# Filling the slot table of a mixture-of-experts kernel: 64 indirect scatters to device memory, or one-hot products summed on TensorE

## What is computed

```python
s_raw_MN = x_MD @ Wg_DN                                   # 8192 tokens x 8 logits
routed = softmax(s_raw_MN[:, :7]);  shared = softmax(s_raw_MN[:, 7:])
_, idx_MK = lax.top_k(routed, 1)                           # one routed expert per token
mask = sum(one_hot(idx_MK, 7), axis=1)
sel = routed * mask;  routed_n = sel / sum(sel, axis=-1)   # its gate
gates = concatenate([routed_n, shared / sum(shared)])
for each expert e:                                         # w1: 256 x 1024, w2: 512 x 256
    a, b = split(x_MD @ w1[e]);  y += gates[:, e] * ((silu(b) * a) @ w2[e])
x = x + gb * y
```

## Time and profile before

| what | value |
|---|---|
| median of three runs | 3036.81 us |
| the profiled execution's own time | 3036.99 us |
| its span in the profile | 3035.2 us |
| busy: PE, DVE, POOL, ACT | 75%, 67%, 65%, 44% of the span |
| last store of `shared_program` issued | 2466.2 us after the start of the span |
| first instruction of DVE in `routing_program` | 2469.96 us |
| first copy of `cur` in `experts_program` | 2579.56 us |

### The profile page before, as it was taken

One profiled execution on the slowest core, in us unless ns is written; L12 is line 12 of the kernel. 1 busy time (PEld: TensorE's weight loads), 2 busy tenths in 40 slices (PEclk: granted clock), 3 DMA queues, 4 the chain that ended last, 5 costly groups with the idle time before them and its releaser, 6 DMA issues. The chain is left out here.

```text
span 3035.2 us, 29143 instructions
## 1 busy us (share of the span) xinstructions
PE 2270.4 (75%) x7448; PEld 1053.1 (35%) x7449; DVE 2030.8 (67%) x2297; ACT 1321.1 (44%) x2151; POOL 1980.8 (65%) x816
## 2 busy tenths in 40 slices
PE   4677687687687786786786785349889940899998
PEld 3223233233232232232232231125555520565664
DVE  3298998998998898988988989924444440122222
ACT  1465565565565665655655655402222210222221
POOL 0189989989889889899898899900000017455553
PEclk7778788787787787787787786669999975999999
DMA  3333433433333434334333333151111100222221
GB/s 109 74 74 75 97 81 73 98 84 73 88 79 81 91 78 90 81 71 101 79 80 91 88 82 85 36 215 63 48 55 62 62 22 2 83 84 86 83 87 51
DMA packets 113435, 238.40 MB, mean 79 GB/s; under 512 B 21516, under 2 KB 75534, under 8 KB 100752
## 3 DMA queue, kind: packets, MB, share of 16 engines
q1 hardware_dynamic: 93328, 189.86, 25.7%
q0 software_dynamic: 14368, 36.00, 4.1%
q10 hardware_dynamic: 5600, 11.01, 1.0%
HBM read 106.10 MB, written 39.20 MB: 48 GB/s over the span
## 5 line engine op out<-in xcount | busy, mean ns | idle before, releaser
L721 POOL TENSOR_TENSOR hs<-hs,c_rep 128x2048 f32<-128x2048 f32 x256 | 1154.6, 4525 | 69.4 <-ACT state L560 69.2
L555 ACT ACTIVATE dA<-d_rep,a 128x512 f32<-128x512 f32 x1024 | 683.6, 686 | 621.8 <-DVE hs L641 618.0
L641 DVE TENSOR_TENSOR_SCAN hs<-dA,state,hs 128x512 f32<-128x512 f32 x768 | 914.6, 1263 | 27.1 <-ACT dA L555 25.9
L714 POOL TENSOR_TENSOR hs<-u_rep,b_rep 128x2048 f32<-128x2048 f32 x96 | 433.6, 4516 | 104.7 <-PE y_ps L437 97.4
L628 DVE TENSOR_TENSOR hs<-u_ps,b_rep 128x2048 f32<-128x2048 f32 x160 | 364.6, 2280 | 135.9 <-PE u_ps L427 135.5
L396 PE MATMUL bank<-xin,w_in 128*128 128x512 f32 x512 | 342.9, 826 | 91.2 <-ACT xpad L491 86.3
L437 PE MATMUL y_ps<-hs,gather 128*32 128x512 f32 x2048 | 275.4, 686 | 142.1 <-POOL hs L721 142.1
L407 PE MATMUL bank<-xdbl,w_dt 65*128 65x512 f32 x256 | 181.5, 847 | 174.9 <-DVE delta L617 117.8
L641 DVE TENSOR_TENSOR_SCAN hs<-dA,hs 128x512 f32<-128x512 f32 x256 | 289.8, 1202 | 12.0 <-ACT dA L555 12.0
L822 POOL TENSOR_TENSOR rstd<-var,mhalf 128x4 f32<-128x4 f32 x16 | 16.1, 1007 | 411.2 <-DVE var L924 411.2
L427 PE MATMUL u_ps<-us,spread 32*128 32x512 f32 x320 | 222.2, 782 | 72.8 <-POOL us L704 62.0
(11 more groups left out here) (169 smaller groups left out, 2646.9 us busy)
## 6 DMA issues: line engine op xcount, KB each, us to landing
d_rep<-delta SPq DMA_DIRECT2D x256, 256.0 KB, 4.3
u_rep<-us SPq DMA_DIRECT2D x384, 64.0 KB, 2.2
b_rep<-bc_rows SPq DMA_DIRECT2D x64, 256.0 KB, 4.4
c_rep<-bc_rows SPq DMA_DIRECT2D x64, 256.0 KB, 7.3
xin<-in_x SPq DMA_DIRECT2D x16, 512.0 KB, 3.8
xres<-in_x SPq DMA_DIRECT2D x16, 512.0 KB, 3.6
x<-xres SPq DMA_DIRECT2D x16, 512.0 KB, 4.4
x_sb<-x SPq DMA_DIRECT2D x16, 512.0 KB, 4.3
```

Of the source, the lines that this page charges most:

```text
L555: nc.scalar.activation(dA[:, u % ABANK, :], d_rep[:, q % 2, j, :], ACT.Exp, scale=t["a"][:, u:u + 1]).then_inc(da_ready, 1)
L641: nc.vector.tensor_tensor_scan(hs[:, s % RING, g, :], dA[:, u % ABANK, :], hs[:, s % RING, g, :], state[:, u:u + 1] if m else 0.0, ALU.mul ...
L714: nc.gpsimd.tensor_tensor(hs[:, s % RING], u_rep[:, i % UBUF, :].unsqueeze(1).to_broadcast([P, NG, T]), b_rep[:, par, :].rearrange("p (g t ...
L721: nc.gpsimd.tensor_tensor(hs[:, s % RING, :, :], hs[:, s % RING, :, :], c_rep[:, par, :].rearrange("p (g t) -> p g t", g=NG), ALU.mult).th ...
```

## The change

Nothing of the list in device memory is left: not its tensor, nor the store of empties (L812), its wait and the two memsets in `shared_program`, nor the 64 scatters and the load in `routing_program`. In their place:

- DVE makes two one-hot tiles of each column of tokens: `at_lane`, 128x128 (row p is 1 at the lane of the slot of token p), and `at_tile`, 128x70 (1 at its slot tile). `sel` holds `at_tile` times the token number plus one, made by DVE, and `at_tile` times the gate, made by ACT (64 activations with the gate as a scale): 128x140 together. This goes in eight groups of `GR` = 8 columns: DVE has three instructions per group, 128x560, 128x1024 and 128x560.
- PE sums `at_lane`, as weights, times `sel` over the 64 columns in one bank of PSUM (`placed`, 128x2x70): lane by slot tile, token number plus one and gate. A group's products begin when both `id_ready` (DVE) and `gate_ready` (ACT) have come to it.
- DVE makes `meta` from `placed`, in five instructions instead of three. An empty slot has 0 there and becomes `EMPTY`.

The chain ahead is written anew with the same results. The first true entry of each token comes from one running sum over 448 elements that is set back to zero at each token (`keep_e`) and one comparison, in place of 13 instructions. `one`, `prefix` and `total` are laid out expert by expert, so that the sums over the columns are one scan of 448 elements (`keep_j` sets it back) instead of seven of 64, and `more` is one instruction instead of seven. `total` is multiplied first and signals alone. `owner` moves behind the eight groups and takes three instructions instead of eight.

```diff
 shared_program
-            sp.wait_ge(empty_set, 2)
-            sp.dma_start(slots_dram.rearrange("(p k) w -> p k w", p=P), empty[:]).then_inc(slots_set, 16)
-            sp.wait_ge(slots_set, 16)
...
-            nc.gpsimd.memset(empty[:, :, 0], EMPTY).then_inc(empty_set, 1)
-            nc.gpsimd.memset(empty[:, :, 1], 0).then_inc(empty_set, 1)
...
 routing_program, gpsimd
             nc.gpsimd.memset(below[:], 1.0).then_inc(tri, 1)
+            nc.gpsimd.memset(keep_e[:], 1.0).then_inc(tri, 1)
+            nc.gpsimd.memset(keep_j[:], 1.0).then_inc(tri, 1)
...
-            pool.wait_ge(slots_ready, 1)
-            pool.wait_ge(consts, 5)
-            for j in range(NTILE):
-                nc.gpsimd.indirect_dma_start(slots_dram, bass.IndirectOffsetOnAxis(slot[:, j:j + 1], 0), info[:, j, :], None).then_inc(scattered, 16)
-        @block.sync
-        def _(sp):
-            sp.wait_ge(scattered, 16 * NTILE)
-            sp.dma_start(slots[:], slots_dram.rearrange("(p k) w -> p k w", p=P)).then_inc(loaded, 16)
-            sp.wait_ge(loaded, 16)
...
 scalar, behind the exponential
+            for g in range(NGRP):
+                act.wait_ge(at_ready, g + 1)
+                for j in range(GR * g, GR * g + GR):
+                    last = nc.scalar.activation(sel[:, j, 1, :], at_tile[:, j, :], ACT.Copy, scale=gate[:, j:j + 1])
+                last.then_inc(gate_ready, 1)
...
 tensor
-            nc.tensor.matmul(flat(prefix), below[:], flat(one), start=True, stop=True)
             nc.tensor.matmul(flat(total), ones[:], flat(one), start=True, stop=True).then_inc(counted, 1)
+            nc.tensor.matmul(flat(prefix), below[:], flat(one), start=True, stop=True).then_inc(counted, 1)
+            for j in range(NTILE):
+                if j % GR == 0:
+                    pe.wait_ge(id_ready, j // GR + 1)
+                    pe.wait_ge(gate_ready, j // GR + 1)
+                last = nc.tensor.matmul(flat(placed), at_lane[:, j, :], sel[:, j].rearrange("p a b -> p (a b)"),
+                                        start=(j == 0), stop=(j == NTILE - 1))
+            last.then_inc(all_placed, 1)
...
 vector
-            link(v.tensor_copy(taken[:], mask[:, :, 0]))
-            link(v.tensor_copy(one[:, :, 0], mask[:, :, 0]))
-            for e in range(1, NR - 1):
-                link(v.tensor_tensor(one[:, :, e], mask[:, :, e], taken[:], ALU.is_gt))
-                link(v.tensor_tensor(taken[:], taken[:], mask[:, :, e], ALU.max))
...
+            dve.wait_ge(consts, 8)
+            link(v.tensor_tensor_scan(flat(cum), flat(keep_e), flat(mask), 0.0, ALU.mult, ALU.add))
+            v.scalar_tensor_tensor(out=one[:].rearrange("p e j -> p j e"), in0=cum[:], scalar=1.0, in1=mask[:],
+                                   op0=ALU.is_equal, op1=ALU.mult).then_inc(onehot, 1)
...
+            link(v.tensor_tensor_scan(flat(incl), flat(keep_j), flat(total), 0.0, ALU.mult, ALU.add))
+            link(v.tensor_tensor(more[:], by_expert(each128), incl[:, :, NTILE - 1:NTILE].to_broadcast([P, NR, NTILE]), ALU.is_lt))
...
+            link(v.tensor_reduce(pos[:], part[:].rearrange("p e j -> p j e"), AX_X, ALU.add))
...
+            for g in range(NGRP):
+                at = slice(GR * g, GR * g + GR)
...
+                v.tensor_tensor(at_tile[:, at], among(kidx, SLOT_TILES), spread(tile, SLOT_TILES), ALU.is_equal).then_inc(at_ready, 1)
+                v.tensor_tensor(at_lane[:, at], among(lanes, P), spread(lane, P), ALU.is_equal)
+                dve.wait_ge(at_ready, g + 1)
+                v.tensor_tensor(sel[:, at, 0, :], at_tile[:, at], spread(id1, SLOT_TILES), ALU.mult).then_inc(id_ready, 1)
...
+            dve.wait_ge(all_placed, 1)
+            link(v.tensor_scalar(empty[:], placed[:, 0, :], 0.5, float(EMPTY), ALU.is_lt, ALU.mult))
+            link(v.scalar_tensor_tensor(out=meta[:, :, 2], in0=placed[:, 0, :], scalar=-1.0, in1=empty[:], op0=ALU.add, op1=ALU.add))
+            link(v.tensor_scalar(meta[:, :, 0], meta[:, :, 2], float(BATCH * SEQ - 1), None, ALU.min))
+            link(v.tensor_copy(meta[:].bitcast(F32)[:, :, 3], placed[:, 1, :]))
```

More of the change, by code:

```diff
@@ L1000, in routing_program @@
[L1000 to L1003 removed]
+        ex, p, mask, cum, work = (sb(n, [P, NTILE, NR]) for n in ("ex", "prob", "mask", "cum", "work"))
@@ new lines, in routing_program @@
+        keep_e, keep_j = sb("keep_e", [P, NTILE, NR]), sb("keep_j", [P, NR, NTILE])
+        nt, tend, base, own, reach = sb("nt", [P, NR]), sb("tend", [P, NR]), sb("base", [P, NR]), sb("own", [P, SLOT_TILES]), sb("reach", [P, SLOT_TILES, NR])
+        at_lane = sb("at_lane", [P, NTILE, P])
+        at_tile, sel = sb("at_tile", [P, NTILE, SLOT_TILES]), sb("sel", [P, NTILE, 2, SLOT_TILES])
+        empty = sb("empty", [P, SLOT_TILES])
+        prefix, total = (ctx.enter_context(nc.psum_tensor(n, [P, NR, NTILE], F32)) for n in ("prefix", "total"))
@@ L1093, in _ @@
             link(v.tensor_scalar(base[:], base[:], float(P), None, ALU.mult))
[L1095 to L1099 removed]
+            link(v.tensor_tensor(part[:], incl[:], total[:], ALU.subtract))
```

88 lines of the change are left out of this document (41 added, 47 removed).

## The result

The changed kernel takes **2970.73 us** (median of four runs, 2970.52 to 2972.13), the kernel before 3036.80 (3034.68 to 3037.05) beside it: ratio 0.9786, interval 0.9775 to 0.9798. That is 66 us less. The forecast was 2969.8. The profiled execution's own time is 2970.52, against a forecast of 2970.0.

A forecast was written before the change was run, and what follows sets the result against it. The serial chain from the shared expert's last stores through list to `cur` bounds it. Parts 1 to 4 save 5.7 us; with the table, `cur` moves 67.0 earlier: 3036.99 to 2970.0, median-adjusted 2969.8; range 2965.5 to 2977.5.

The forecast's parts named there:

- Part 1: Start of the routing block: removing the store of empties gives 0.2 us, at most 0.43; five more POOL constants cost nothing.
- Part 2: One-hot choice on DVE: one scan and one wide instruction, 4.27 to 2.04 us, with 0.28 per 256-byte jump.
- Part 3: Gate: `total` signals alone, so DVE's wait for PE goes; 3.48 becomes 2.40 us, 1.08 less.
- Part 4: Counts, from the scan of `total` to the table: 10.34 becomes 8.12 us, small instructions at 0.265 each.
- Part 5: Table: DVE sets the pace at 2.41 us per group (bound 2.81), ACT 2.05, PE 2.18; before, it took 84.0.
- start at half clock: PE's first table group at half clock takes 3.94 us, later ones 2.18; PE catches up 0.23 per group.
- rival in which the clock stays at half through all products: PE sets the table's pace at 3.94 us per group: 12.3 us more, 2982.1; 9 in 100.
- `meta` to `cur`: From the finished table to the experts' first POOL instruction: 1.62 us, unchanged.
- The experts: Routed experts, from first `cur` to the end: 455.6 us as before; another value would show the forecast wrong.
- term that it left out: PE's clock staying up until the experts' first transpose: taken as nothing, bound 2.0 us less.
- ACT's pace: Rival: ACT sets the table's pace at 3.0 us per group; 4.9 us more, 2974.7; 8 in 100.
- table loads: Slower rival: ACT loads its table ahead of each copy, 1.54 us per copy; 3049 us; 1 in 100.

The follow-up runs named there:

- warm variant: The changed kernel plus nine spare 448-column products on PE ahead of the table, which nobody reads; 2971.13 us, ratio 0.9784.
- spare DMA: The changed kernel plus one unread GpSimd indirect gather of 128 rows in the routing block, issued early (2969.89 us) or, in a second run, late (2966.2 us).
- extra drain: The changed kernel with smaller last groups and one GpSimd drain behind the routed experts' last gather; 2960.65 us, ratio 0.9753.
- small groups, warm: The changed kernel with groups of 8 (six times), 6, 4, 3 and 3 columns, plus nine spare PE products ahead of the table; 2971.51 us.
- table alone: The changed kernel with the old chain (expert by expert, both products ahead of the signal), one-hot table kept; 2974.77 us, ratio 0.9802.

## Why the prediction was right

**What bounds it**: right. The list was all that the experts waited for; every us of the serial stretch came off the whole.

**Part 1**, 0.2: measured 0.25, of which the store alone is 0.16. The five constants more were free: the last began at 2473.06, three us ahead of DVE's scan at 2476.11. Even the margin was larger than thought, since the `affine_select` takes 0.29 now, not 0.71.

**Part 2**, 2.04: measured 2.08. The scan of 448 took 1.09 (1.07 forecast). The open question was whether a *write* with a jump of 256 bytes pays what a read does. It does: 0.92 for `one` (L1078) and 0.93 for its reader, where the unjumped kind takes 0.62 to 0.63. (L1078 is of another kind than the products, SCALAR_TENSOR_TENSOR, but at 128x512 the kernel before has this kind at 680 ns, L617, and the product at 687, L963.) The Trainium skill's rule (SBUF — State Buffer, "Door 1: The DMA port swizzle"), by which every access that crosses to a new line pays, agrees in all three places, L1099's 0.91 among them.

**Part 3**, 2.40: measured 2.46. DVE no longer waits for `total`.

**Part 4**, 8.12: measured 7.76. The mis-sized term are the small instructions: 0.265 each was forecast, while they stand 0.20 to 0.23 apart.

**Part 5.** The group: 2.41 forecast, 2.44 measured (0.65 + 1.14 + 0.65 from start to start, where the records are 0.73, 1.22 and 0.73 long). The choice between 2.41 and 2.81 was made by the pair of the earlier trace rows, and the trace bears it out. The Trainium skill's rule (VectorE: DVE Perf Modes, "The DRAIN you can't avoid") would have had 2.81 by its main sentence, that the next instruction waits until the pipe is empty; the same section adds that one that is not held starts earlier, which the prediction left out. The trace agrees with the addition: unlinked instructions begin some 0.08 us before the one ahead has ended.

ACT: eight copies 2.05 forecast, 2.06 measured, though for another reason than I gave: one copy's record is 339 ns, near the upper price of 0.345, but they start 0.245 apart. The gain of running on, which the prediction named, is there (0.09 per copy), and it cancels what the record is longer than forecast. That the scale is what makes the record longer no run shows, since none has the same copy without it. ACT stays 0.38 under DVE.

PE: 2.18 per group at full clock. A group with a pause ahead of it takes 2.15, but groups that follow each other without a pause start only 1.91 apart (2498.26, 2500.17, 2502.08). The other step that was mis-sized is the **start at half clock**. "I take the first group at half", 4.0 us. The windows (PE, weights, DVE, ACT and POOL busy; granted clock; DMA):

```profile
2491.40:2497.40 6.00, 6.00 (x26) 6.00 (x27) 6.00 (x8) 5.01 (x20) 0.00 (x0) 0.50 0.00 1
2497.50:2508.00 10.50, 10.50 (x88) 10.31 (x86) 10.50 (x15) 8.98 (x37) 0.00 (x0) 1.00 0.00 0
```

The clock stood at 0.50, 1.2 GHz, for 6 us after 9.8 us in which PE had been idle, and then went to 1.00, 2.4 GHz. In the variants it rose 3.6 to 6 us behind the first product, with no cause that the rows tell apart. 26 records went through at half clock instead of 16. So PE was behind by 2.5 us instead of 1.8 (3.94 - 2.18), but caught up 0.53 per group (2.44 - 1.91) instead of 0.23. By the prediction's own price of a group the later rise would have lain on the path; that it did not is luck, two mis-sized terms against each other. The warm variant shows that it cost nothing: same end. Had the table been two groups shorter, 0.3 us would have been on PE's path, by the debt left behind the sixth group. The rival in which the clock stays at half through all products did not come: ahead of the last group and in the warm variant there are pauses of 0.3 us, and the clock stays at 1.00.

The wait of DVE for `placed`, "1 us": 1.19. `owner` was hidden.

**`meta` to `cur`**, "1.62, which stays": this step failed. (1.62 is itself 0.03 short: `meta`'s last row ends at 2577.91, not 2577.94.) It was 0.53, and the missing 1.1 was GpSimd's drain after 64 scatters. The prediction had looked at every instruction that was removed, and not at what the barrier behind it was waiting for.

**The experts**, 455.6: 456.16. The first gather takes 1.23 instead of 1.01 now that no scatter goes ahead of it; before, the first scatter had paid this (1.29 in the earlier trace rows). The spare DMA that took this away brought no fall that could be told from the spread of the stretch over versions with the same code, 455.00 to 456.71. The kept traces show what goes with that spread: PE's granted clock is at 0.50 when the experts start and rises to 1.00 some 13 to 16 us behind `cur`, and over the thirteen traces without the extra drain the stretch grows by 0.50 us for each us that the rise comes later. The ends are 455.0 with the rise 12.9 behind `cur` (small groups, warm) and 456.7 with 16.5 (table alone). Before, it came 14.35 behind `cur`, after, 15.58: 0.6 us by this slope, which is all of the 0.5. So by its own sign, "if the experts' stretch is not 455.6", the prediction was off here by 0.5, by a moment of the clock that no row explains. The term that it left out, a clock that stays up until the first transpose, was nothing, as it took: between 2520 and 2525 the granted clock was 0.50.

So the 0.9 us between forecast and result is partly luck. Chain 0.3 and `meta` to `cur` 1.1 better; table 0.3, experts 0.5 and the store 1.27 worse. These sum to -1.4 + 2.1 = +0.7, and the forecast had rounded `cur` up by 0.1: the 0.5 us by which the profiled time missed, within rounding. The largest two, the drain at 1.1 and the store at 1.27, nearly cancel, and neither was foreseen. Of the rivals, ACT's pace (a group of 3.0) and table loads (none: each copy 0.339) are excluded by the rows above.

## What to carry to other kernels

A long row of small indirect DMAs that builds a table costs 1.27 us each on GpSimd's queue, and one-hot products give the same table at 2.44 us for eight columns of 128 tokens; with several engines in a relay, only the slowest counts, and PE at half clock at the start is free as long as the groups that follow are enough to work off what it is behind. When work is taken from an engine, ask also what the next barrier waited for: GpSimd's drain at a block's end grows with the indirect DMAs since the last one, and a drain placed where GpSimd is idle took 8.7 us off the end of this kernel. Don't put an elementwise product on GpSimd beside a busy DVE before looking at DVE's own rows: here one of DVE's two instructions took twice as long, and the group as a whole 0.27 longer, with one instruction less on DVE.

## What the runs showed of the hardware that I had not expected

- **GpSimd's drain** after 1 indirect DMA 0.142 us, after 4 0.385, after 24 2.03, after 210 9.28 to 9.30, each time behind a wait for their landing. It is not proportional (0.08 each at 24, 0.044 at 210); why, no run tells. The 24 were small gathers, the others wide gathers and stores, and no run holds the kind fixed.
- **DVE beside GpSimd**: a 128x560 product with two inputs in SBUF took 1.54 us in the mean instead of 0.73 while GpSimd made one of the same shape in 2.03.
- **Indirect DMAs in the routing block**: GpSimd took 1.93 and 3.16 us for the spare gather of 128 rows beside the table's instructions, where the experts' gather of such rows takes 0.98; the 24 small ones took 0.94 to 1.69. What slows them no run tests.
- **A jump of 256 bytes** costs a DVE instruction of 448 elements 0.28 to 0.31 us, written as well as read.
- **The rise of PE's clock** from 0.50 to 1.00 (1.2 to 2.4 GHz) came 3.6 to 6.1 us behind the table's first product in versions with nearly the same instruction order, and 12.9 to 16.5 behind the first `cur` in the experts, where each us of delay went with 0.5 more.
